# Unrolled gathers and a nine-instruction combine in the last stage of an attention and mixture-of-experts kernel

## The reference, cut to what matters

```python
x = x + attn(layernorm(x))
x = x + ffn(layernorm(x))

def ffn(x):                                   # x: [4096, 128]
    probs = sigmoid(x @ router_w.T + expert_bias)
    top_w, top_idx = top_k(probs, 8)
    top_w = top_w / (sum(top_w) + 1e-9) * 2.5
    h1 = silu(einsum('th,eih->eti', x, w_gate))
    routed = einsum('eti,ehi->th', h1 * combine.T[:, :, None], w_down)
    shared = silu(x @ w_gate_shared.T) @ w_down_shared.T
    return routed + shared
```

## Time and profile before

| | |
|---|---|
| median of 3 runs | 1271.67 us (1271.46 to 1271.88) |
| the profiled execution | 1268.07 us |
| its span in the trace | 1266.2 us |
| busy: PE, DVE, ACT, POOL | 963.0, 735.0, 775.7, 698.8 us |
| first and last gather start | 762.7 and 1258.2 us |

### The profile page before, as it was taken

One profiled execution on the slowest core, in us unless ns is written; L12 is line 12 of the kernel. 1 busy time (PEld: TensorE's weight loads), 2 busy tenths in 40 slices (PEclk: granted clock), 3 DMA queues, 4 the chain that ended last, 5 costly groups with the idle time before them and its releaser, 6 DMA issues.

```text
span 1266.2 us, 30672 instructions
## 1 busy us (share of the span) xinstructions
PE 963.0 (76%) x8800; PEld 723.2 (57%) x8800; DVE 735.0 (58%) x2510; ACT 775.7 (61%) x2405; POOL 698.8 (55%) x892
## 2 busy tenths in 40 slices
PE   5999999999999999999996594575655755756600
PEld 4777777777777777777774373353433533434400
DVE  4578887878787878788884373142323413423442
ACT  6888888778787878888875274473433523634500
POOL 2237666666667666766675404424445355354375
PEclk9999999999999999999996696685666756766755
DMA  8536544444422121222223374463434534434321
GB/s 288 226 136 236 213 176 162 166 159 157 162 95 93 58 87 60 95 74 73 93 106 118 126 252 139 120 194 114 145 101 132 152 106 120 154 115 130 109 79 52
DMA packets 75561, 169.99 MB, mean 134 GB/s; under 512 B 13808, under 2 KB 23984, under 8 KB 75504
## 3 DMA queue, kind: packets, MB, share of 16 engines
q1 hardware_dynamic: 56816, 133.63, 30.0%
q0 software_dynamic: 16384, 33.59, 9.3%
q10 hardware_dynamic: 2304, 2.10, 0.5%
HBM read 66.50 MB, written 102.76 MB: 134 GB/s over the span
## 4 chain that ended last, share of the span: by engine, by line
PE 54%; another core or an unknown queue 14%; issue 12%; ACT 7%; DVE 5%; POOL 4%; DMA 2%; ACTq 1%; DVEq 0%; POOLq 0%; SPq 0%
PE psS L433 9%; PE psO L508 9%; PE psT L458 7%; PE psY L424 7%; PE psA L470 4%; PE psVM L424 4%; POOL yg L949 3%; PE psS L619 3%; PE psT L607 3%; DMA block_y<-y_b 2%; PE psO L630 2%; ACT p_sb L730 2%; ACT w_b L791 2%; PE psY L630 1%
## 5 line engine op out<-in xcount | busy, mean ns | idle before, releaser
L949 POOL DMA_INDIRECT yg<-block_y,tok_idx x256 | 246.2, 962 | 289.1 <-issue 159.1
L921 POOL DMA_INDIRECT slot_x<-xn_src,slot_u x240 | 244.6, 1019 | 99.1 <-issue 53.1
L730 ACT ACTIVATE p_sb<-psS,negmax 128x256 f32<-128x256 f32 x512 | 235.8, 475 | 84.7 <-DVE negmax L1278 83.6
L1319 DVE COPY w_b<-w_all 128x192 f32 x497 | 96.5, 259 | 279.5 <-remote 202.6
L883 POOL TENSOR_SCALAR p_sb<-p_sb,rinv 128x256 f32<-128x256 f32 x256 | 137.4, 544 | 134.1 <-DVE rinv L1227 129.5
L1278 DVE TENSOR_REDUCE negmax<-psS 128x2 f32<-128x512 f32 x256 | 163.9, 681 | 28.4 <-PE psS L433 28.2
L508 PE MATMUL psO<-pT_sb,v_sb 128*64 128x256 f32 x1024 | 138.8, 390 | 21.7 <-ACT pT_sb L306 10.8
L433 PE MATMUL psS<-qk_sb 64*128 64x256 f32 x1024 | 145.2, 402 | 2.7 <-ACT p_sb L730 2.3
L306 ACT COPY pT_sb<-psT 128x512 f32<-128x512 f32 x256 | 140.3, 612 | 2.3 <-PE psT L458 2.3
L607 PE MATMUL psT<-ident,xb 128*128 128x128 f32 x416 | 89.9, 351 | 61.7 <-issue 40.6
L458 PE MATMUL psT<-ident,p_sb 128*128 128x128 f32 x1024 | 132.8, 273 | 0.4 <-POOL p_sb L883 0.4
(11 more groups left out here) (172 smaller groups left out, 1984.9 us busy)
## 6 DMA issues: line engine op xcount, KB each, us to landing
block_y<-zero SPq DMA_DIRECT2D x26, 1024.0 KB
xb<-slot_x SPq DMA_DIRECT2D x104, 256.0 KB
block_y<-y_b SPq DMA_DIRECT2D x104, 256.0 KB
slot_x<-zero SPq DMA_DIRECT2D x15, 1024.0 KB
w_all<-in_wgd_dram SPq DMA_DIRECT2D x16, 960.0 KB
slot_x<-zero SPq DMA_DIRECT2D x1, 11264.0 KB, 41.4
yg<-block_y,tok_idx POOLq DMA_INDIRECT x256
slot_x<-xn_src,slot_u POOLq DMA_INDIRECT x240
```

The lines of the kernel that those rows point to most:

```text
L730: act.activation(p_sb[:, (g - 1) % 2, h, qt, :], psS[:, h, qt * SEQ:(qt + 1) * SEQ], ACT.Exp, bias=negmax[:, (g - 1) % 2, h, qt:qt + 1], s ...
L921: pool.indirect_dma_start(slot_x, bass.IndirectOffsetOnAxis(ap=slot_u[:, int(last), i, j:j + 1], axis=0), (xn2 if last else xn2_src)[:, i, ...
L949: pool.indirect_dma_start(yg[:, r, k, :], None, block_y, bass.IndirectOffsetOnAxis(ap=tok_idx[:, par, r, k:k + 1], axis=0)).then_inc(gat[r ...
```

## The change

On POOL the hardware loop of the gathers is gone: all 32 tiles are written out, every wait is on a constant, and the gathers read their row numbers from pos_u directly, so that tok_idx, its eight copies and idx_cp are gone. A gather of tile n waits for acc_ok of tile n-4, which DVE sends at the end of the combine, where it had been ys_ok, sent one instruction before the end.

On DVE a tile is combined by nine instructions on 128 columns each. Four of them (scalar_tensor_tensor) add the rows 0, 2, 4, 6, each times its weight, into x_res in place, in a chain on the semaphore even_ok. Between them a tensor_scalar and three scalar_tensor_tensor build the rows 1, 3, 5, 7 in acc, in a chain on odd_ok. The ninth adds both. The waits for the output store of tile n-4 and for the shared expert's part (shared_ok) stand ahead of the first. The last eight combines are written out.

```diff
-            def gather(n, b, par, r):
-                if not isinstance(n, int) or n >= YR:
-                    wait_apart(pool, s["ys_ok"], n - YR + 1)
...
-                        wait_apart(pool, sty[k], 8 * NGRP if late else 8 * SEQ_BLK // GB * b + 8 * (E + SEQ_BLK) // GB)
...
-                                            bass.IndirectOffsetOnAxis(ap=tok_idx[:, par, r, k:k + 1], axis=0)).then_inc(gat[r], 16)
+            def gather(n):
+                r, b = n % YR, n // TB
+                wait(pool, s["acc_ok"], n - YR + 1)
...
+                        pool.wait_ge(sty[k], 8 * NGRP if b >= SEALED else 8 * SEQ_BLK // GB * b + 8 * (E + SEQ_BLK) // GB)
                 for k in range(TOPK):
                     pool.indirect_dma_start(yg[:, r, k, :], None, block_y,
+                                            bass.IndirectOffsetOnAxis(ap=pos_u[:, n, k:k + 1], axis=0)).then_inc(gat[r], 16)
...
-            with pool.Fori(1, NT // YR // 2 - 1) as i:
...
+            for n in range(NT):
+                gather(n)
...
-                dve.tensor_tensor(yg[:, r], yg[:, r], w, ALU.mult).then_inc(s["yw_ok"], 1)
...
-                dve.tensor_tensor(acc[:, r, :], yg[:, r, 0, :], yg[:, r, 1, :], ALU.add).then_inc(s["ys_ok"], 1)
...
+                xr, odd = x_res[:, n, :], acc[:, r, :]
+                dve.wait_ge(gat[r], 16 * TOPK * (n // YR + 1))
+                dve.wait_ge(s["shared_ok"], n // TB + 1)
+                wait(dve, sto[r], 16 * (n // YR))
+                for k in range(0, TOPK, 2):
+                    wait(dve, s["even_ok"], TOPK // 2 * n + k // 2)
+                    dve.scalar_tensor_tensor(out=xr, in0=yg[:, r, k, :], scalar=wE_res[:, n, k:k + 1], in1=xr, op0=ALU.mult,
+                                             op1=ALU.add).then_inc(s["even_ok"], 1)
+                    w = wE_res[:, n, k + 1:k + 2]
+                    if k == 0:
+                        dve.tensor_scalar(odd, yg[:, r, 1, :], w, None, ALU.mult).then_inc(s["odd_ok"], 1)
+                    else:
+                        dve.wait_ge(s["odd_ok"], TOPK // 2 * n + k // 2)
+                        dve.scalar_tensor_tensor(out=odd, in0=yg[:, r, k + 1, :], scalar=w, in1=odd, op0=ALU.mult,
+                                                 op1=ALU.add).then_inc(s["odd_ok"], 1)
...
+                dve.tensor_tensor(odd, odd, xr, ALU.add).then_inc(s["acc_ok"], 1)
```

More of the change, by code:

```diff
@@ L230, in build @@
         blk_i = sb("blk_i", [P, NBLK], I32)
-        tok_idx = sb("tok_idx", [P, 2, YR, TOPK], U32)
         w_all = sb("w_all", [P, E, INTER + D])
@@ L258, in build @@
                 w_cp wa_cp xt2_ps xt2_ok g_ps h_ok y_ps y_ok
-                idx_cp sh_ps hs_ok sho_ps shared_ok yw_ok y4_ok y2_ok ys_ok acc_ok""".split():
+                sh_ps hs_ok sho_ps shared_ok even_ok odd_ok acc_ok""".split():
             s[name] = sem(name)
@@ L930, in _ @@
             pool.wait_ge(s["scat_l"], 16 * (NT - SEALED * TB) * TOPK)
-            def slots_of(n, par):
-                pool.tensor_copy(tok_idx[:, par], pos_u[:, bass.ds(n, YR), :]).then_inc(s["idx_cp"], 1)
-            def gather(n, b, par, r):
-                if not isinstance(n, int) or n >= YR:
-                    wait_apart(pool, s["ys_ok"], n - YR + 1)
-                if isinstance(n, int) and n == 2:
+            def gather(n):
+                r, b = n % YR, n // TB
+                wait(pool, s["acc_ok"], n - YR + 1)
+                if n == 2:
                     pool.wait_ge(s["wr_ok"], B)
                     pool.wait_ge(s["po_ok"], B)
-                if r % TB == 0:
-                    late = isinstance(b, int) and b >= SEALED
+                if n % TB == 0:
                     for k in range(2):
-                        wait_apart(pool, sty[k], 8 * NGRP if late else 8 * SEQ_BLK // GB * b + 8 * (E + SEQ_BLK) // GB)
+                        pool.wait_ge(sty[k], 8 * NGRP if b >= SEALED else 8 * SEQ_BLK // GB * b + 8 * (E + SEQ_BLK) // GB)
                 for k in range(TOPK):
                     pool.indirect_dma_start(yg[:, r, k, :], None, block_y,
-                                            bass.IndirectOffsetOnAxis(ap=tok_idx[:, par, r, k:k + 1], axis=0)).then_inc(gat[r], 16)
[L952 to L964, removed]
-            with pool.Fori(1, NT // YR // 2 - 1) as i:
[L966 to L969, removed]
+                                            bass.IndirectOffsetOnAxis(ap=pos_u[:, n, k:k + 1], axis=0)).then_inc(gat[r], 16)
+            for n in range(NT):
+                gather(n)
         @block.vector
@@ L1320, in weights_of, with combine @@
                 m.then_inc(s["w_cp"], 1)
-            def combine(n, q, r):
-                dve.wait_ge(gat[r], 16 * TOPK * (q + 1))
-                w = wE_res[:, bass.ds(n, 1), :].rearrange("p o k -> p (o k)").unsqueeze(2).broadcast_to([P, TOPK, D])
-                dve.tensor_tensor(yg[:, r], yg[:, r], w, ALU.mult).then_inc(s["yw_ok"], 1)
[L1327 to L1333, removed]
-                dve.tensor_tensor(acc[:, r, :], yg[:, r, 0, :], yg[:, r, 1, :], ALU.add).then_inc(s["ys_ok"], 1)
-                dve.wait_ge(s["ys_ok"], n + 1)
-                dve.tensor_tensor(acc[:, r, :], acc[:, r, :], x_res[:, bass.ds(n, 1), :].rearrange("p o d -> p (o d)"),
-                                  ALU.add).then_inc(s["acc_ok"], 1)
+            def combine(n):
+                r = n % YR
+                xr, odd = x_res[:, n, :], acc[:, r, :]
[13 more added lines that the diff above has]
+                                                 op1=ALU.add).then_inc(s["odd_ok"], 1)
+                dve.wait_ge(s["even_ok"], TOPK // 2 * (n + 1))
+                dve.wait_ge(s["odd_ok"], TOPK // 2 * (n + 1))
+                dve.tensor_tensor(odd, odd, xr, ALU.add).then_inc(s["acc_ok"], 1)
@@ L1393, in _ @@
                 for n in range(TILES_BY[j], TILES_BY[j + 1]):
[L1394 to L1397, removed]
+                    combine(n)
+            for n in range(TILES_BY[-1], NT):
+                combine(n)
 _OUTS = [((B, SEQ, D), "float32")]
```

## The result

The changed kernel takes 1297.45 us (median of 4 runs, 1294.5 to 1298.92) against 1271.57 of the kernel before (4 runs, 1269.18 to 1271.88): 1.022 of it, 95% interval 1.019 to 1.024. It is slower, where I forecast 1257.2, and outside the range. The profiled execution took 1298.92, its span is 1297.1.

The account below looks back on a forecast made before the run. A chain of waits, gather bursts alternating with groups, sets the pace from 838 to 1200 us, then POOL alone. Gains 9.7 + 2.4 + 0.6 + 1.8 = 14.5 us off 1271.67 give 1257.2 us, range 1245 to 1272.

Parts of the forecast that it names:

- The wake-up: POOL's gathers start 0.27 us after the combine instead of 1.14 or 0.78, joints inside bursts shrink: 9.7 us gained.
- The combine: DVE's combine before the next burst takes 2.58 us instead of 2.73: 2.4 us over 16 starts, last combine 0.6.
- Gathers held by DVE: Nine POOL gathers prolonged by long DVE instructions, 3.7 us excess; half counted gone with short instructions: 1.8 us gained.
- the sum: All gains together: 9.7 + 2.4 + 0.6 + 1.8 = 14.5 us.
- The step that failed: From 838 to 1200 us bursts and groups take turns, so savings before the next burst shorten the kernel; 14.5 us in all.
- The prediction's own sign for being wrong: Wrong if time from a burst's end to the next start does not shrink by about 1 us on average.
- The first rival: Earlier bursts catch one more y_b store, moving a 2.5 us group behind the burst; nine times gives 1279.7; chance 0.14.

Follow-up runs that it names:

- B: Condition of some runs: kernel before, unchanged, takes 1056 to 1058 us; the changed kernel measured there 0.986 of it.
- A: Condition of the first measurement and some later runs: kernel before, unchanged, takes 1269 to 1284 us; the changed kernel first measured 1.022 of it.

## Why the prediction was wrong, step by step

**The wake-up** was right where it was read: 0.27 us after the combine's end, and no gap over 0.39. In B it is paid, by 6.8 us instead of the 9.7 that I took from trace A. In A the half that holds it seems to cost time, by the quotient 1.015 above; it was not run alone there.

**The combine** was right: starts 0.26 us apart (I took 0.27), 2.51 us in all (2.58). The prediction had weighed a rule of the Trainium skill ("VectorE: DVE Perf Modes", section "The DRAIN you can't avoid"), that an instruction does not start until the pipe is empty. The same paragraph goes on that a next one which is not held starts earlier, and the prediction left that out. The trace shows this second case for alternating chains: instructions of 0.34 us start 0.26 apart.

**Gathers held by DVE** went, all but one of 1.28 us; 1.8 us was too little for condition B, where 9.3 us lay in them. So in B the sum came out near 14.5 although its two main terms had changed size.

**The step that failed** is the one that made all terms count: that the time from a burst's end to the next start shrinks by what is taken from the combine and the wake-up. Under it lay a reading that was wrong: "While a burst runs, the stores of y_b do not get through." They do, within 2.3 us in the middle of a burst; the copies waited for PE. The step was argued from one pair of bursts, in which a group got through just behind a start. The time behind a burst is not a fixed chain: it holds as many groups as the burst has left over, three in the changed kernel where it had mostly been two. One more of them costs more than the 1.2 us that the earlier start saves; net of that, the cycles of 16 grew by 2.9 on average. The prediction's own sign for being wrong, that this time does not shrink by about 1 us, is what the traces show.

**The first rival** forecast the pattern that came, a group moved from beside the burst to behind it, and I gave it 0.14. Its mechanism, a store that is stuck, was wrong, so that the pattern fits is in part luck. Its price of one group, 2.5 us, was below the 3.4 that each of the eight cycles lost on average, and its count of 9 near those 8 (six of 16 and two of 8). It was held too small because I set the margin of the start against a store. The store is not the cause: PE itself slows, here 2.35 us into the burst. And that side of the burst's start had been read nowhere: the earlier trace rows show a copy 1.6 us behind a start, at 1053.87, in a burst that starts at 1052.27; of seven bursts of 16 before, six had such a catch or a pause, and listing them all would have shown that an earlier start had catches to lose and none to win. The rival's time of 1279.7 also left out the tail, 4.1 us, and gave the gains in full, of which the traces show none in the middle.

**What stays open.** Why PE's matmuls come singly and its signals late during gathers in condition A and not in B; that no instructions are transferred in these bursts speaks against late instructions but does not settle it. How much of the loss of the six catches and pauses is the earlier start (P) and how much the missing pauses (J). What makes condition A. No version beats both kernels in both conditions: in B the changed kernel is the best that was run (its loops written out change nothing), in A the kernel before.

## What to carry to other kernels

When two kinds of work take turns, count the work that slips in at every seam before you move one of them: a wait that is taken out can move the seam to where nothing slips in. A stretch in which an engine waits for nothing that the profile shows is a warning that the trace may be of one condition of several; run both kernels side by side again before believing either sign. Where an engine slows beside indirect gathers, pauses between them may not be all waste; here that is a guess from a few cycles. And a wait that the profile puts down to "remote" is not yet a store: look whether the store's packets had moved.

## What the runs showed of the hardware

The same program took 1057 us or 1270 to 1284, on the same chip by its number, with the same DMA bytes and packets. The granted clock was 0.92 and 0.84, but most of the difference lies in the last stage: the kernel before gathered from 712.3 to 1049.3 us in the one and from 762.7 to 1259.1 in the other. In condition A, in the burst shown, PE ran clean for 2.35 us after the start of gathers and then issued 26 matmuls in 15 us, and its signal for a group came 7.5 us after the group's last matmul (1019.01 and 1026.53). SP's store of 256 KB, issued in the middle of a burst, had moved 1.7 us later (1027.22 to 1028.9). A scalar_tensor_tensor on 128x128 took 0.34 us and the next, of another chain, started 0.26 later. A gather that started beside a two-input DVE instruction on 1024 or 512 columns lasted up to 1.97 us; beside the short ones none was over 1.28.
